# Pairwise interaction tower on one core: products stored so that both halves of the embedding share partitions, an accumulating DMA per group of products, and one column sum in TensorE instead of two

## The chip, the cores and the metric

The kernel runs on 1 core of one Trainium2 chip. The metric is device time in microseconds, the median of several runs. TensorE (PE) multiplies matrices, VectorE (DVE) does the elementwise products, ScalarE (ACT) copies out of PSUM, GpSimd (POOL) and SyncE (SP) issue DMAs, which 16 DMA engines carry out.

## The reference, cut to what matters

```python
e = jnp.stack([tbl_0[ids[:, 0]], ..., tbl_39[ids[:, 39]]], axis=1)   # 512 x 40 x 64
vi, vj = e[:, i_idx, :], e[:, j_idx, :]                              # all 780 pairs i < j
viW = jnp.einsum('bpd,pde->bpe', vi, W)                              # W: 780 x 64 x 64
z = jnp.einsum('bpe,bpe->bp', viW, vj)                               # 512 x 780
h = jnp.concatenate([z, dense_ctx], axis=1)                          # + 16
h = jnp.maximum(h @ W_top1 + b_top1, 0.0)                            # 796 -> 512
h = jnp.maximum(h @ W_top2 + b_top2, 0.0)                            # 512 -> 256
y = h @ W_top3                                                       # 256 -> 1
```

All is float32. For each pair of fields the kernel forms W'e_i, multiplies it elementwise by e_j and sums over the 64 dimensions of the embedding.

## The kernel before, in words

The batch of 512 lies along the free axis everywhere. The 40 fields are taken as 20 pairs of fields. The pair of fields 2k and 2k+1 is called k, and u = 19 - k is the order in which they arrive. `E[:, k, :]` holds both, transposed: one field on partitions 0 to 63 and the other on 64 to 127.

The first two arrivals are looked up on TensorE with one-hot codes (small tables). The other 18 are fetched by POOL, with eight indirect DMAs each (2 fields x 4 slices of the batch), into a ring of four buffers `rows`. TensorE transposes them into `ps_e` (L388), and ACT copies `ps_e` to `E` (L288).

The 780 pairs are packed into 100 groups of 8 pairs (a few with gaps). A group has two steps. A step is two matmuls (L408, `products`) from 64 partitions of `w_sb` and `E` into two banks of `ps_t`. The two run side by side, on the upper and the lower half of the array. Each gives 128 rows: two pairs of fields with 64 dimensions each. `ps_t` has room for STEPS = 3 steps. DVE multiplies each step by `E` into `prod` (L355, `multiply`), one instruction of 128 x 1024.

The sum over the embedding is then a matmul with a matrix of ones and zeros (L420, `reduce`): four matmuls of 128 rows and 32 columns per group, one for each 512 columns of `prod`, which go side by side to the four quarters of the partitions of `ps_z`. Sixteen groups fill a chunk of `ps_z`, which ACT copies to `z`. There are 7 chunks, the last of 4 groups.

The order of the work on TensorE is a list written by `order()`: after the products of every odd group n, `reduce(n-3)` and `reduce(n-2)` follow, and the transposes of an arrival stand one group ahead of the first group that needs it. SP loads weights (`w_sb`, 256 KB for two groups, ring of 12) and the parameters of the top layers. POOL does nothing but the gathers. After the last group the top layers run on TensorE (L446, L464, L470), with the last two reductions among the matmuls of L446.

Of the kernel before, what the change touches and what calls it, by code (L numbers as in the profile page):

```python
# [16 lines left out]
DIM = 64  # L34
DENSE = 16
PAIRS = FIELDS * (FIELDS - 1) // 2
KP = FIELDS // 2
SP_ = KP // 2
# [7 lines left out]
G_RING = 4  # L46
W_RING = 12
P_RING = 4
STEPS = 3


def pair(i, j):

    return i * FIELDS - i * (i + 1) // 2 + j - i - 1


def plan_groups():


    groups = []  # L60
    for k in reversed(range(KP)):
        for M in range(k // 2 + 1, SP_):
            groups.append((k, [(i, (pair(i, 2 * m), pair(i, 2 * m + 1)), m)
                               for m in (2 * M, 2 * M + 1) for i in (2 * k, 2 * k + 1)]))
        if k % 2 == 0:

            own = [(2 * k, (None, pair(2 * k, 2 * k + 1)), k),
                   (2 * k + 3, (pair(2 * k + 2, 2 * k + 3), None), k + 1)]
            cross = [(i, (pair(i, 2 * k + 2), pair(i, 2 * k + 3)), k + 1) for i in (2 * k, 2 * k + 1)]
            groups.append((k, own + cross))  # L70

    groups.insert(3, groups.pop(0))
    return groups
# [10 lines left out]
AHEAD = 1  # L84
PARAMS_AT = 12


def arrival(k):

    return KP - 1 - k  # L90


def first_group(u):

    return next((n for n, (k, _) in enumerate(GROUPS) if arrival(k) >= u), NG)
# [6 lines left out]
def place(u):  # L102

    return SPLIT_FIRST.index(u) if u < FIRST else u


def order():

    u = 0
    for n in range(NG):  # L110
        while u < KP and first_group(u) - AHEAD <= n:
            yield "fields", u
            u += 1
        yield "group", n


def table_split(rows):

    used = max(d for d in range(1, P + 1) if rows % d == 0)
    return used, rows // used  # L120


def tower_kernel(nc, w_units, ids, ids_by_field, tables, dense, w1, b1, w2, b2, w3, out):
    with ExitStack() as ctx:
# [15 lines left out]
        halves = sb("halves", [P, 2 * (2 * PER_CHUNK - 1)])  # L140
# [3 lines left out]
        prod = sb("prod", [P, P_RING, BLOCKS, BATCH])  # L144

        scratch = prod[:].rearrange("p a b n -> p (a b n)")
# [41 lines left out]
        halves_zeroed = sem("halves_zeroed")  # L188
        halves_ready = sem("halves_ready")
        rows_loaded = [sem(f"rows_loaded{i}") for i in range(G_RING)]  # L190
        transposed = sem("transposed")
        e_copied = sem("e_copied")
        w_loaded = [sem(f"w_loaded{i}") for i in range(W_RING)]
        step_done = sem("step_done")
        product_ready = sem("product_ready")
        group_reduced = sem("group_reduced")
# [10 lines left out]

# [46 lines left out]
        @block.gpsimd  # L254
        def _(pool):
            pool.memset(ident[:], 0.0).then_inc(ident_zeroed, 1)
            pool.wait_ge(ident_zeroed, 1)
            pool.affine_select(out=ident[:], in_=ident[:], compare_op=ALU.not_equal, fill=1.0, base=0,
                               pattern=[[-1, P]], channel_multiplier=1).then_inc(ident_ready, 1)
            for i, f in enumerate(looked_up):  # L260
                pool.iota(first_row[:, i:i + 1], pattern=[[0, 1]], base=0,
                          channel_multiplier=splits[f][1]).then_inc(first_row_ready, 1)
            pool.wait_ge(ids_loaded, 16)

            def gather(u):
# [12 lines left out]
            for u in range(LOOKED_UP, KP):  # L278
                gather(u)

        @block.scalar
        def _(act):
            def copy_fields(u):
                if u < LOOKED_UP:
# [3 lines left out]
                act.activation(E[:, KP - 1 - u, :], e_bank[u], ACT.Copy).then_inc(e_copied, 1)  # L288

            def copy_z(c):  # L290
                if c < CHUNKS - 1:
                    act.wait_ge(group_reduced, PER_CHUNK * (c + 1))
                    act.activation(z[:, c, :], ps_z[:], ACT.Copy).then_inc(z_copied, 1)  # L293
                else:
                    act.wait_ge(group_reduced, NG)
                    top = 32 * (BLOCKS - 1)
                    act.activation(z[0:top, c, :], ps_z[0:top, :], ACT.Copy).then_inc(z_copied, 1)
# [3 lines left out]
            for kind, at in order():  # L301
                if kind == "fields":
                    if at >= FIRST:
                        copy_fields(at)
                elif at % 2 == 1 and (at - 1) % PER_CHUNK == 0 and at > 1:
                    copy_z(at // PER_CHUNK - 1)
            copy_z(CHUNKS - 1)
# [11 lines left out]
        def _(dve):  # L319
            dve.memset(halves[:], 0.0).then_inc(halves_zeroed, 1)  # L320
            mid = 2 * (PER_CHUNK - 1)
            dve.wait_ge(halves_zeroed, 1)
            dve.memset(halves[0:DIM, mid:mid + 1], 1.0).then_inc(halves_ready, 1)
            dve.memset(halves[DIM:P, mid + 1:mid + 2], 1.0).then_inc(halves_ready, 1)

# [5 lines left out]

# [10 lines left out]
            def multiply(n):  # L342
                slot = n % P_RING
                if n >= P_RING:
                    dve.wait_ge(group_reduced, n - P_RING + 1)
                blocks = GROUPS[n][1]
                for s in range(2):
                    m0, m1 = blocks[2 * s][2], blocks[2 * s + 1][2]
                    dve.wait_ge(e_copied, max(place(arrival(m)) for m in (m0, m1)) + 1)
                    dve.wait_ge(step_done, 2 * n + s + 1)  # L350
                    if m0 == m1:
                        multiplier = E[:, m0, None, :].to_broadcast([P, 2, BATCH])
                    else:
                        multiplier = E[:, m0:m0 + 2, :]
                    dve.tensor_tensor(prod[:, slot, 2 * s:2 * s + 2, :], ps_t[:, (2 * n + s) % STEPS, :, :], multiplier,  # L355
# [6 lines left out]
            dve.wait_ge(group_reduced, NG)  # L362
# [5 lines left out]
        def _(pe):  # L368
            def look_up_fields(u):

                before = sum(len(codes_of) for codes_of in code_list[:u])
                for j, (f, c) in enumerate(code_list[u], start=before):
                    if u == 1 and j - before in FETCHED_AT:
                        transpose_fields(LOOKED_UP + FETCHED_AT.index(j - before))
                    if c == 0:
# [3 lines left out]
                    last = pe.matmul(e_bank[u][half:half + DIM, :], small[f][:, c, :],  # L379
                                     codes[0:splits[f][0], j % CODE_RING, :],  # L380
                                     start=(c == 0), stop=(c == splits[f][1] - 1)).then_inc(code_used, 1)
# [10 lines left out]
            def products(n):  # L392
# [3 lines left out]
                k, blocks = GROUPS[n]  # L396
                pe.wait_ge(e_copied, max(place(arrival(i // 2)) for i, _, _ in blocks) + 1)
                for s in range(2):
                    step = 2 * n + s

# [4 lines left out]
                    for j in range(2):  # L405
                        i = blocks[2 * s + j][0]
                        at, col = i % 2 * DIM, (n % 2 * 2 + s) * P
                        last = pe.matmul(ps_t[:, step % STEPS, j, :], w_sb[at:at + DIM, m % W_RING, col:col + P],  # L408
                                         E[at:at + DIM, i // 2, :], start=True, stop=True)
                    last.then_inc(step_done, 1)  # L410

            def reduce(n):

                pe.wait_ge(product_ready, 2 * n + 2)
                c, q = divmod(n, PER_CHUNK)
                if c >= 1 and q == 0:
                    pe.wait_ge(z_copied, c)
                at = 2 * (PER_CHUNK - 1 - q)
                for b in range(BLOCKS):
                    last = pe.matmul(ps_z[32 * b:32 * b + 32, :], halves[:, at:at + 32],  # L420
                                     prod[:, n % P_RING, b, :], start=(q == 0),
                                     stop=(q == PER_CHUNK - 1 or n == NG - 1))
                last.then_inc(group_reduced, 1)

            pe.wait_ge(ident_ready, 1)
            pe.wait_ge(halves_ready, 2)
            for u in range(LOOKED_UP):
                look_up_fields(u)
            for kind, at in order():
# [9 lines left out]
            pe.wait_ge(params_loaded, 16 * (CHUNKS + 5))  # L439
            pe.wait_ge(z_copied, CHUNKS - 1)  # L440
            pe.wait_ge(e_copied, KP)
# [33 lines left out]
def z_rows():  # L475

    at = np.full((CHUNKS, P), -1)
    for n, (_, blocks) in enumerate(GROUPS):
        for b, (_, halves, _) in enumerate(blocks):
            for h, p in enumerate(halves):  # L480
                if p is not None:
                    at[n // PER_CHUNK, 32 * b + 2 * (n % PER_CHUNK) + h] = p
    at[CHUNKS - 1, DENSE_AT:DENSE_AT + DENSE] = PAIRS + np.arange(DENSE)
    return at
# [42 lines left out]
```

## Time and profile before

| | |
|---|---|
| median of 3 runs | 361.19 us (360.8 to 361.52) |
| the profiled execution, its own time | 361.39 us |
| its span, first to last instruction | 359.4 us |
| granted clock of TensorE | 1.000 |
| PE busy | 343.5 us (96%) |
| DVE busy | 249.4 us (69%) |
| POOL busy | 139.4 us (39%) |
| ACT busy | 22.1 us (6%) |

Busy time is the time in which at least one instruction of the engine ran; one matmul of float32 stands as two records. The span is some 2 us shorter than the time that is measured. Windows and timelines count from the first instruction.

### The profile page before, as it was taken

To read this page: it belongs to the slowest core of one execution; us is meant where nothing else is said; L and a number is where in the kernel's file an instruction comes from. 1 tells how busy PE (TensorE), PEld (TensorE's weight loads), DVE (VectorE), ACT (ScalarE), POOL (GpSimd) and SP (SyncE) were. 2 spreads that over 40 slices of the span, in tenths; PEclk is the share of its full clock that TensorE was granted. 3 is DMA by queue.
4 is the path that set the end of the run, shared out by engine and by line. 5 is a ranking of instruction groups with operands and counts; after the bars stand their busy time and mean duration, and the time that the engine had idled before them with its cause. 6 is when DMAs were issued, how large, how long until landed. Compare 5 with 4: busy or idle time off the path is not lost.

```text
span 359.4 us, 4510 instructions
## 1 busy us (share of the span) xinstructions
PE 343.5 (96%) x1824; PEld 117.6 (33%) x1824; DVE 249.4 (69%) x243; ACT 22.1 (6%) x35; POOL 139.4 (39%) x154
## 2 busy tenths in 40 slices
PE   0799998999999999999999999999999999999997
PEld 0233332333332333333333333333333332333342
DVE  2384977687879787878888788787878979870000
ACT  1011000000000000000000000000000000000032
POOL 6777777777777777772343500000000000000000
DMA  6972222222233239322131220212000000000000
GB/s 167 256 215 63 83 57 58 83 60 84 55 86 63 80 96 308 88 55 75 40 78 45 71 60 29 60 30 60 29 0 2 0 2 0 0 3 0 0 2 0
DMA packets 14399, 22.87 MB, mean 64 GB/s; under 512 B 3750, under 2 KB 3878, under 8 KB 14379
## 3 DMA queue, kind: packets, MB, share of 16 engines
q1 hardware_dynamic: 9770, 17.86, 16.5%
q0 software_dynamic: 4608, 4.73, 6.2%
q8 instruction: 15, 0.25, 0.3%
q14 instruction: 6, 0.04, 0.0%
HBM read 22.57 MB, written 0.00 MB: 63 GB/s over the span
## 4 chain that ended last, share of the span: by engine, by line
PE 80%; POOL 13%; issue 4%; DMA 1%; DVE 1%; ACT 0%; DVEq 0%
PE ps_t L408 45%; PE ps_z L420 24%; POOL rows L273 13%; PE ps_t L446 5%; PE ps_e L388 2%; PE ps_t L464 2%; PE ps_e L446 2%; DVE prod L355 1%; DMA rows<-in_tbl,ids_sb 1%; DMA ids_sb<-in_ids_t 1%; PE ps_t L470 1%; ACT y_sb L316 0%; DVEq L350 0%
## 5 line engine op out<-in xcount | busy, mean ns | idle before, releaser
L355 DVE TENSOR_TENSOR prod<-ps_t,E 128x1024 f32<-128x1024 f32 x200 | 231.7, 1216 | 60.1 <-PE ps_t L408 58.9
L408 PE MATMUL ps_t<-E,w_sb 64*128 64x512 f32 x800 | 189.2, 606 | 0.2
L273 POOL DMA_INDIRECT rows<-in_tbl,ids_sb x144 | 138.4, 961 | 63.9 <-issue 43.0
L408 PEld LDWEIGHTS ps_t<-E,w_sb 64*128 64x128 f32 x800 | 69.5, 186 | 109.7 <-issue 80.0
L420 PE MATMUL ps_z<-prod,halves 128*32 128x512 f32 x800 | 96.4, 598 | 0.0
L420 PEld LDWEIGHTS ps_z<-prod,halves 128*32 128x32 f32 x800 | 20.8, 109 | 68.0 <-DVE prod L355 34.9
L288 ACT ACTIVATE E<-ps_e 128x512 f32<-128x512 f32 x18 | 10.8, 598 | 231.7 <-PE ps_e L388 209.7
L338 DVE TENSOR_SCALAR prod<-prod,first_row_f 125x512 f32<-125x512 int32 x38 | 16.5, 495 | 11.8 <-PE ps_e L379 5.8
L379 PE MATMUL ps_e<-prod 125*64 125x512 f32 x40 | 12.8, 728 | 11.2 <-DMA prod<-in_tbl 11.2
L446 PE MATMUL ps_t<-z,w_sb 128*128 128x512 f32 (+1 forms) x42 | 18.7, 597 | 0.0
L388 PE MATMUL ps_e<-ident,rows 128*128 128x128 f32 x68 | 11.1, 286 | 2.3 <-DMA rows<-in_tbl,ids_sb 2.3
L364 DVE COPY z<-ps_z 8x512 f32<-8x512 f32 x1 | 0.7, 697 | 17.6 <-PE ps_z L420 17.6
L388 PEld LDWEIGHTS ps_e<-ident,rows 128*128 128x128 f32 x68 | 7.1, 141 | 15.8 <-issue 10.9
L446 PEld LDWEIGHTS ps_t<-z,w_sb 128*128 128x128 f32 (+1 forms) x42 | 7.8, 190 | 10.8 <-issue 10.8
L379 PEld LDWEIGHTS ps_e<-prod 125*64 125x64 f32 x40 | 3.5, 166 | 19.6 <-issue 14.3
L379 PE MATMUL ps_t<-prod 125*64 125x512 f32 x36 | 9.0, 596 | 0.0
L293 ACT ACTIVATE z<-ps_z 128x512 f32<-128x512 f32 x6 | 3.6, 597 | 66.6 <-PE ps_z L420 66.6
L464 PE MATMUL ps_t<-E,w_sb 128*128 128x512 f32 x16 | 7.0, 592 | 0.0
L446 PE MATMUL ps_e<-z,w_sb 128*128 128x512 f32 (+1 forms) x14 | 6.4, 600 | 0.0
L464 PEld LDWEIGHTS ps_t<-E,w_sb 128*128 128x128 f32 x16 | 3.0, 190 | 3.8 <-issue 3.8
L379 PEld LDWEIGHTS ps_t<-prod 125*64 125x64 f32 x36 | 2.7, 137 | 4.9 <-issue 3.5
L446 PEld LDWEIGHTS ps_e<-z,w_sb 128*128 128x128 f32 (+1 forms) x14 | 2.6, 190 | 3.7 <-issue 3.7
(22 smaller groups left out, 12.6 us busy)
## 6 DMA issues: line engine op xcount, KB each, us to landing
w_sb<-in_w_units SPq DMA_DIRECT2D x50, 256.0 KB, 2.6
rows<-in_tbl,ids_sb POOLq DMA_INDIRECT x144, 2.5
w_sb<-in_w SPq DMA_DIRECT2D x7, 256.0 KB
prod<-in_ids_by_field SPq DMA_DIRECT2D x2, 512.0 KB, 9.0
prod<-in_tbl SPq DMA_DIRECT2D x3, 312.5 KB
w_sb<-in_w SPq DMA_DIRECT2D x1, 512.0 KB
prod<-in_tbl SPq DMA_DIRECT2D x1, 250.0 KB
ids_sb<-in_ids_t SPq DMA_DIRECT2D x1, 80.0 KB, 1.8
```

What stands on the lines that cost most here:

```text
L273: pool.indirect_dma_start(rows[:, g % G_RING, b, f * DIM:(f + 1) * DIM], None, tables[2 * k + f], bass.IndirectOffsetOnAxis(ap=ids_sb[:, c ...
L288: act.activation(E[:, KP - 1 - u, :], e_bank[u], ACT.Copy).then_inc(e_copied, 1)
L293: act.activation(z[:, c, :], ps_z[:], ACT.Copy).then_inc(z_copied, 1)
L338: dve.tensor_scalar(codes[0:used, j % CODE_RING, :], ids_wide[0:used, i, :], float(c), first_row_f[0:used, i:i + 1], ALU.subtract, ALU.is_ ...
L355: dve.tensor_tensor(prod[:, slot, 2 * s:2 * s + 2, :], ps_t[:, (2 * n + s) % STEPS, :, :], multiplier, ALU.mult).then_inc(product_ready, 1)
L379: last = pe.matmul(e_bank[u][half:half + DIM, :], small[f][:, c, :], codes[0:splits[f][0], j % CODE_RING, :], start=(c == 0), stop=(c == s ...
L388: last = pe.transpose(e_bank[u][:, b * P:(b + 1) * P], rows[:, (u - LOOKED_UP) % G_RING, b, :], ident[:])
L408: last = pe.matmul(ps_t[:, step % STEPS, j, :], w_sb[at:at + DIM, m % W_RING, col:col + P], E[at:at + DIM, i // 2, :], start=True, stop=True)
L420: last = pe.matmul(ps_z[32 * b:32 * b + 32, :], halves[:, at:at + 32], prod[:, n % P_RING, b, :], start=(q == 0), stop=(q == PER_CHUNK - 1 ...
L446: last = pe.matmul(h1_bank[m], w1_sb[0:used, c, m * P:(m + 1) * P], z[0:used, c, :], start=(c == 0), stop=(c == CHUNKS - 1))
L464: last = pe.matmul(h2_bank[m], w2_sb[:, c, m * P:(m + 1) * P], h1[:, c, :], start=(c == 0), stop=(c == H1 // P - 1))
L470: last = pe.matmul(y_bank[0:1, :], w3_sb[:, c:c + 1], h2[:, c, :], start=(c == 0), stop=(c == H2 // P - 1))
```

## The change

The products are laid out anew. For an ordinary group (k, M), which pairs the fields 2k and 2k+1 with the four fields 4M to 4M+3, step 0 now makes dimensions 0 to 31 of all four products, and step 1 dimensions 32 to 63, on the same 128 partitions. So the two halves of a product stand at the same partitions of `prod[:, slot, 0]` and `prod[:, slot, 1]`. The multiplier must have the same layout, so a new tensor `E4` is filled from `E` by four small DMAs (32 partitions x 2 KB) per arrival, issued by ACT behind its copy. `E` itself becomes a ring of 6.

For 76 of the 100 groups (`ADDED`: ordinary ones from 10 to 91), POOL issues an accumulating DMA that adds half 1 to half 0 in `prod`, 512 KB read and added to 512 KB. TensorE then sums only `prod[:, slot, 0]`: two matmuls for the group and not four. The groups (k, None), which hold the pairs within a block of four fields, keep the old layout and sums, as does TensorE for the groups outside `ADDED` (two sums each).

Reductions are now taken by two groups at a time (`reduce_two`), so that the matmuls of two groups stand side by side in the four quarters of `ps_z`. Both being in `ADDED` (35 of the 50 twos), four matmuls do; else (6 twos with one in it, 9 with none) a second round for half 1 follows. `reduce_two(n-7)` follows the products of odd n (before: n-3 and n-2), and `prod` has 8 slots for 4. POOL's gathers are issued between the adds, twelve groups ahead.

```diff
-P_RING = 4
+P_RING = 8
+LAG = 7
+GATHER_LEAD = 12
+ADDED = [n for n, (_, M) in enumerate(GROUPS) if M is not None and 10 <= n < 92]
...
-        E = sb("E", [P, KP, BATCH])
+        E = sb("E", [P, E_RING, BATCH])
+        E4 = sb("E4", [P, QUADS, 2, BATCH])
...
-            for u in range(LOOKED_UP, KP):
-                gather(u)
+            def add_halves(n):
+                pool.wait_ge(product_ready, 2 * n + 2)
+                pool.dma_start(prod[:, n % P_RING, 0, :, :], prod[:, n % P_RING, 1, :, :],
+                               accum_op=ALU.add).then_inc(halves_added[n % P_RING], 16)
+
+            u = LOOKED_UP
+            for n in range(NG):
+                while u < KP and first_group(u) <= n + GATHER_LEAD:
+                    gather(u)
+                    u += 1
+                if n in ADDED:
+                    add_halves(n)
...
-                act.activation(E[:, KP - 1 - u, :], e_bank[u], ACT.Copy).then_inc(e_copied, 1)
+                if u >= E_RING:
+                    act.wait_ge(product_ready, 2 * last_group(u - E_RING) + 2)
+                    act.wait_ge(e4_placed[u - E_RING], 64)
+                act.activation(E[:, slot_of(k), :], e_bank[u], ACT.Copy).then_inc(e_copied, 1)
+                if k < 2:
+                    return
+                act.wait_ge(e_copied, place(u) + 1)
+                for f in range(2):
+                    for h in range(2):
+                        to, of = (2 * (k % 2) + f) * HALF, f * DIM + h * HALF
+                        act.dma_start(E4[to:to + HALF, k // 2, h, :], E[of:of + HALF, slot_of(k), :]).then_inc(
+                            e4_placed[u], 16)
...
-                    if at > 1 and at % 2 == 1:
-                        reduce(at - 3)
-                        reduce(at - 2)
+                    if at >= LAG and at % 2 == 1:
+                        reduce_two(at - LAG)
...
+            def reduce_two(n):
+                c, q = divmod(n // 2, PER_CHUNK // 2)
+                if c >= 1 and q == 0:
+                    pe.wait_ge(z_copied, c)
+                for g in (n, n + 1):
+                    pe.wait_ge(product_ready, 2 * g + 2)
+                    if g in ADDED:
+                        pe.wait_ge(halves_added[g % P_RING], 16 * sum(a % P_RING == g % P_RING for a in ADDED if a <= g))
+                for s in range(2):
+                    for g in (n, n + 1):
+                        if s == 1 and g in ADDED:
+                            continue
+                        if GROUPS[g][1] is None:
+                            ones = halves[:, 30 - 4 * q - 2 * s:62 - 4 * q - 2 * s]
+                        else:
+                            ones = quads[:, 28 - 4 * q:60 - 4 * q]
+                        for j in range(2):
+                            to = 32 * (2 * (g % 2) + j)
+                            last = pe.matmul(ps_z[to:to + 32, :], ones, prod[:, g % P_RING, s, j, :],
+                                             start=(q == 0 and s == 0),
+                                             stop=((q == PER_CHUNK // 2 - 1 or n == NG - 2)
+                                                   and (s == 1 or g in ADDED)))
+                last.then_inc(two_reduced, 1)
...
-            sum_h1(0, 0, CHUNKS - 1)
-            reduce(NG - 2)
-            for m in range(1, 3):
-                sum_h1(m, 0, CHUNKS - 1)
-            reduce(NG - 1)
-            for m in range(3, H1 // P):
+            reduce_two(NG - 6)
+            pe.wait_ge(params_loaded, 16 * (CHUNKS + 5))
+            pe.wait_ge(z_copied, CHUNKS - 2)
+            pe.wait_ge(e_copied, KP)
+            sum_h1(0, 0, CHUNKS - 2)
+            reduce_two(NG - 4)
+            sum_h1(0, CHUNKS - 2, CHUNKS - 1)
+            pe.wait_ge(product_ready, 2 * NG - 2)
+            sum_h1(1, 0, CHUNKS - 1)
+            reduce_two(NG - 2)
+            for m in range(2, H1 // P):
                 sum_h1(m, 0, CHUNKS - 1)
```

The first groups are reordered, too: (16, None) and (18, None) now stand first; they don't read `E4`. An arrival u is first needed by group 16 (u = 8), 20 (u = 9), 25 (u = 10), and so on to 90 (u = 19), as before.

## Rows read from the trace of the kernel before

**Rows 1.** The page: busy time, share of the span and instructions of each engine.

```profile
PE 343.5 (96%) x1824; PEld 117.6 (33%) x1824; DVE 249.4 (69%) x243; ACT 22.1 (6%) x35; POOL 139.4 (39%) x154
```

**Rows 2.** The chain that ended last, in order of time: start us, us, what.

```profile
64.03 2.34 DMA rows<-in_tbl,ids_sb
...
68.99 1.85 PE ps_z L420 x16
70.84 3.63 PE ps_t L408 x16
...
321.85 5.35 PE ps_e L446 x12
```

**Rows 3.** Groups of instructions by line: out<-in, shapes, count | busy us, mean ns | idle before.

```profile
L355 DVE TENSOR_TENSOR prod<-ps_t,E 128x1024 f32<-128x1024 f32 x200 | 231.7, 1216 | 60.1 <-PE ps_t L408 58.9
L408 PE MATMUL ps_t<-E,w_sb 64*128 64x512 f32 x800 | 189.2, 606 | 0.2
...
L420 PE MATMUL ps_z<-prod,halves 128*32 128x512 f32 x800 | 96.4, 598 | 0.0
```

**Rows 4.** Stretches: length, PE, PEld, DVE, ACT and POOL busy, clock, DMA share, GB/s.

```profile
67.00:100.00 33.00, 33.00 (x195) 11.19 (x196) 25.64 (x23) 2.39 (x4) 25.00 (x27) 1.00 0.27 73
100.00:200.00 100.00, 99.93 (x578) 34.12 (x578) 80.02 (x70) 4.78 (x8) 61.07 (x65) 1.00 0.33 91
200.00:321.80 121.80, 121.74 (x713) 40.46 (x709) 100.47 (x88) 4.19 (x7) 3.09 (x4) 1.00 0.08 24
321.80:359.40 37.60, 35.35 (x96) 13.90 (x92) 1.08 (x2) 5.30 (x8) 0.00 (x0) 1.00 0.00 0
```

**Rows 5.** Timeline around 200 us: start us, us, engine, line, operation, count, idle before.

```profile
204.51 4.62 DVE L355 TENSOR_TENSOR prod<-ps_t,E 128x1024 f32<-128x1024 f32 x4 [0.87 <-PE ps_t L408]
```

**Rows 6.** Timeline of POOL: last gather of u = 7, first of 8, first and last of 9.

```profile
64.03 0.94 POOL L273 DMA_INDIRECT rows<-in_tbl,ids_sb  x1 [0.30 <-issue]
65.27 0.95 POOL L273 DMA_INDIRECT rows<-in_tbl,ids_sb  x1 [0.30 <-issue]
...
75.26 0.94 POOL L273 DMA_INDIRECT rows<-in_tbl,ids_sb  x1 [0.30 <-issue]
...
83.99 0.94 POOL L273 DMA_INDIRECT rows<-in_tbl,ids_sb  x1 [0.30 <-issue]
```

**Rows 7.** Timeline of PE and ACT: products of groups 16 and 17, then a reduction.

```profile
66.41 0.66 PE L388 MATMUL ps_e<-ident,rows 128*128 128x128 f32 x4 [0.85 <-DMA rows<-in_tbl,ids_sb]
...
82.53 3.70 PE L408 MATMUL ps_t<-E,w_sb 64*128 64x512 f32 x16
...
86.17 1.92 PE L420 MATMUL ps_z<-prod,halves 128*32 128x512 f32 x16
```

**Rows 8.** The gathers (min/median/max ns, first to last start) and their landing.

```profile
L273 POOL DMA_INDIRECT rows<-in_tbl,ids_sb x144: 938/944/1305, 2.9 to 203.1; - x144
...
DMA to landing us min/median/max: 2.3/2.5/6.7
```

**Rows 9.** The page: DMA queues, and DMA issues with KB each and us to landing.

```profile
q1 hardware_dynamic: 9770, 17.86, 16.5%
q0 software_dynamic: 4608, 4.73, 6.2%
...
w_sb<-in_w_units SPq DMA_DIRECT2D x50, 256.0 KB, 2.6
```

**Rows 10.** SP's issues of the weights (min/median/max ns).

```profile
L240 SPq DMA_DIRECT2D w_sb<-in_w_units x50: 327/328/3710, 4.2 to 252.8; - x50
```

**Rows 11.** Timeline of the first products: ACT's copy of the last of four arrivals, and DVE.

```profile
34.05 0.60 ACT L288 ACTIVATE E<-ps_t 128x512 f32<-128x512 f32 x1 [1.26 <-PE ps_t L379]
...
35.19 9.14 DVE L355 TENSOR_TENSOR prod<-ps_t,E 128x1024 f32<-128x1024 f32 x8 [4.82 <-PE ps_t L408]
```

More of the change, by code:

```diff
@@ L34 @@
 DIM = 64
+HALF = DIM // 2
 DENSE = 16
@@ L61, in plan_groups @@
     for k in reversed(range(KP)):
-        for M in range(k // 2 + 1, SP_):
-            groups.append((k, [(i, (pair(i, 2 * m), pair(i, 2 * m + 1)), m)
-                               for m in (2 * M, 2 * M + 1) for i in (2 * k, 2 * k + 1)]))
+        groups += [(k, M) for M in range(k // 2 + 1, QUADS)]
         if k % 2 == 0:
[L67 to L73, printed above, removed]
+            groups.append((k, None))
+    first = [(KP - 4, None), (KP - 2, None)]
+    return first + [g for g in groups if g not in first]
 GROUPS = plan_groups()
@@ L81, with pairs_of, last_group @@
 DENSE_AT = 32 * (BLOCKS - 1) + LAST_ROWS
-AHEAD = 1
-PARAMS_AT = 12
+ADDED = [n for n, (_, M) in enumerate(GROUPS) if M is not None and 10 <= n < 92]
 def arrival(k):
     return KP - 1 - k
+def pairs_of(n):
+    k, M = GROUPS[n]
+    return [[k, k], [k, k]] if M is not None else [[k + 1, k], [k, k]]
 def first_group(u):
     return next((n for n, (k, _) in enumerate(GROUPS) if arrival(k) >= u), NG)
+def last_group(u):
+    return max(n for n in range(NG) for ks in pairs_of(n) for k in ks if arrival(k) == u)
 SPLIT_FIRST = (0, 2, 3, 1)
@@ L104, in place, with slot_of @@
     return SPLIT_FIRST.index(u) if u < FIRST else u
+def slot_of(k):
+    return arrival(k) % E_RING
 def order():
@@ L192, in tower_kernel @@
         e_copied = sem("e_copied")
+        e4_placed = [sem(f"e4_placed{u}") for u in range(KP)]
         w_loaded = [sem(f"w_loaded{i}") for i in range(W_RING)]
@@ L195, in tower_kernel @@
         product_ready = sem("product_ready")
-        group_reduced = sem("group_reduced")
+        halves_added = [sem(f"halves_added{i}") for i in range(P_RING)]
+        two_reduced = sem("two_reduced")
         z_copied = sem("z_copied")
@@ L304, in _ @@
                         copy_fields(at)
-                elif at % 2 == 1 and (at - 1) % PER_CHUNK == 0 and at > 1:
-                    copy_z(at // PER_CHUNK - 1)
-            copy_z(CHUNKS - 1)
+                elif at % 2 == 1 and at > LAG and (at - LAG + 2) % PER_CHUNK == 0:
+                    copy_z((at - LAG) // PER_CHUNK)
+            copy_z(CHUNKS - 2)
+            act.wait_ge(two_reduced, NU)
+            top = 32 * (BLOCKS - 1)
+            act.activation(z[0:top, CHUNKS - 1, :], ps_z[0:top, :], ACT.Copy).then_inc(z_copied, 1)
             act.wait_ge(params_loaded, 16 * (CHUNKS + 5))
@@ L342, in multiply @@
             def multiply(n):
-                slot = n % P_RING
+                k, M = GROUPS[n]
                 if n >= P_RING:
-                    dve.wait_ge(group_reduced, n - P_RING + 1)
-                blocks = GROUPS[n][1]
-                for s in range(2):
-                    m0, m1 = blocks[2 * s][2], blocks[2 * s + 1][2]
-                    dve.wait_ge(e_copied, max(place(arrival(m)) for m in (m0, m1)) + 1)
-                    dve.wait_ge(step_done, 2 * n + s + 1)
[L351 to L355, printed above, removed]
+                    dve.wait_ge(two_reduced, (n - P_RING) // 2 + 1)
+                if M is None:
+                    dve.wait_ge(e_copied, max(place(arrival(k)), place(arrival(k + 1))) + 1)
+                elif k == 2 * M - 1:
+                    for m in (2 * M, 2 * M + 1):
+                        dve.wait_ge(e4_placed[arrival(m)], 64)
+                for s in range(2):
+                    if M is not None:
+                        multiplier = E4[:, M, s, None, :].to_broadcast([P, 2, BATCH])
+                    elif s == 0:
+                        multiplier = E[:, slot_of(k + 1):slot_of(k + 1) + 2, :]
+                    else:
+                        multiplier = E[:, slot_of(k + 1), None, :].to_broadcast([P, 2, BATCH])
+                    dve.wait_ge(step_done, 2 * n + s + 1)
+                    dve.tensor_tensor(prod[:, n % P_RING, s, :, :], ps_t[:, (2 * n + s) % STEPS, :, :], multiplier,
                                       ALU.mult).then_inc(product_ready, 1)
@@ L378, in look_up_fields @@
                     half = f % 2 * DIM
[L379 to L381 removed]
+                    pe.matmul(e_bank[u][half:half + DIM, :], small[f][:, c, :],
+                              codes[0:splits[f][0], j % CODE_RING, :],
+                              start=(c == 0), stop=(c == splits[f][1] - 1)).then_inc(code_used, 1)
             def transpose_fields(u):
@@ L395, in products @@
                     pe.wait_ge(w_loaded[m % W_RING], 16 * (m // W_RING + 1))
-                k, blocks = GROUPS[n]
-                pe.wait_ge(e_copied, max(place(arrival(i // 2)) for i, _, _ in blocks) + 1)
+                pe.wait_ge(e_copied, max(place(arrival(k)) for ks in pairs_of(n) for k in ks) + 1)
                 for s in range(2):
@@ L410, in products @@
                     last.then_inc(step_done, 1)
-            def reduce(n):
-                pe.wait_ge(product_ready, 2 * n + 2)
-                c, q = divmod(n, PER_CHUNK)
+            def reduce_two(n):
+                c, q = divmod(n // 2, PER_CHUNK // 2)
                 if c >= 1 and q == 0:
                     pe.wait_ge(z_copied, c)
[L418 to L423, printed above, removed]
+                for g in (n, n + 1):
[8 more added lines that the diff above has]
+                            ones = halves[:, 30 - 4 * q - 2 * s:62 - 4 * q - 2 * s]
+                        else:
+                            ones = quads[:, 28 - 4 * q:60 - 4 * q]
[6 more added lines that the diff above has]
+                last.then_inc(two_reduced, 1)
@@ L477, in z_rows, with weight_index @@
     at = np.full((CHUNKS, P), -1)
[L478 to L482, printed above, removed]
-    at[CHUNKS - 1, DENSE_AT:DENSE_AT + DENSE] = PAIRS + np.arange(DENSE)
+    for n, (k, M) in enumerate(GROUPS):
+        for j in range(2):
+            row = at[n // PER_CHUNK, 32 * (2 * (n % 2) + j) + 4 * (n // 2 % (PER_CHUNK // 2)):][:4]
+            if M is not None:
+                row[:] = [pair(2 * k + j, 4 * M + t) for t in range(4)]
+            else:
+                row[1 - j] = pair(2 * k + 2, 2 * k + 3) if j == 0 else pair(2 * k, 2 * k + 1)
+                row[2:] = [pair(2 * k + j, 2 * k + 2), pair(2 * k + j, 2 * k + 3)]
+    at[CHUNKS - 1, DENSE_AT:DENSE_AT + DENSE] = PAIRS + np.arange(DENSE)
+    return at
+def weight_index():
+    d, e = np.arange(DIM)[:, None], np.arange(DIM)[None, :]
+    at = np.full((NG, 2, 2, DIM, P), PAIRS * DIM * DIM)
+    for n, (k, M) in enumerate(GROUPS):
+        for j in range(2):
+            if M is not None:
+                for s in range(2):
+                    for t in range(4):
+                        at[n, s, j, :, t * HALF:(t + 1) * HALF] = (
+                            pair(2 * k + j, 4 * M + t) * DIM * DIM + d * DIM + (e + s * HALF))[:, :HALF]
+            else:
+                for t in range(2):
+                    at[n, 1, j, :, t * DIM:(t + 1) * DIM] = pair(2 * k + j, 2 * k + 2 + t) * DIM * DIM + d * DIM + e
+        if M is None:
+            at[n, 0, 0, :, DIM:] = pair(2 * k + 2, 2 * k + 3) * DIM * DIM + d * DIM + e
+            at[n, 0, 1, :, :DIM] = pair(2 * k, 2 * k + 1) * DIM * DIM + e * DIM + d
     return at
```

59 lines of the change are left out of this document (26 added, 33 removed).

## The prediction, on record before the result was known

> **What bounds the kernel now.** I read the page first: TensorE is busy for 343.5 of 359.4 us, DVE for 249.4, POOL for 139.4 [rows 1]. The stretches say where that holds: from 67 us to the end of the groups at 321.8 us TensorE never rests, DVE is busy for about 80% of it, and POOL is in use only up to 203 us [rows 4, 8]. By line, products and reductions take 189.2 and 96.4 us of TensorE's time [rows 3]; the change thins the second. The chain shows the rhythm: 3.63 us for the products of two groups, 1.85 us for their two reductions, so 5.48 us for two groups [rows 2]. Ahead of 67 us the last thing waited for is a gather (2.34 us from issue to landing, until 66.4) [rows 2, 7]. DVE needs 4.62 us for the four multiplications of two groups, 1.155 us each, and then idles 0.87 us until TensorE has made more [rows 5]. So TensorE is the bound by 0.86 us in every two groups, and DVE stands right behind it. That 0.86 us, not the time of the matmuls taken out, is what a lighter TensorE can give.
>
> **The change part by part.** *The reductions.* Two groups now take 8 matmuls in 1.85 us, which run four abreast: 0.925 us a round. Where both are added (35 twos of 50) one round goes: TensorE needs 3.63 + 0.925 = 4.56 us. DVE needs 4.62, and sets the pace. The twos with one added group or none (15) keep both rounds and 5.48 us. Gain: 35 x (5.48 - 4.62) = 30.1 us. Had TensorE alone set it, 32.4. The three banks of ps_t let DVE run on meanwhile: of 3 x 1.155 = 3.47 us per turn of a bank, DVE's 1.155 and TensorE's 0.91 leave 1.4 us, more than the 0.925 of a round, so I take no bubble.
>
> *The adds on POOL.* A DMA issued by POOL is in the trace only as a gather: 0.94 us and 0.30 us to the next, 1.25 us each [rows 6, 8]. An add also has 128 rows, so I take 1.25 us. Bounds: 0.33 us, what SP spends on a plain issue [rows 10], and 2.5 us, twice a gather, if source and target are each described in two pieces. In all, POOL gets 76 x 1.25 = 95 us on top of its 80 gathers from u = 10 on (100 us).
>
> *Landing.* A 256 KB load lands 2.6 us after issue [rows 9]. On q1 a megabyte takes 0.165 x 16 x 359.4 / 17.86 = 53 us of one engine [rows 9], so a further 256 KB on 16 engines is 0.87 us: an add lands 3.4 to 3.5 us after its issue begins, if it costs as a plain copy.
>
> *First wait.* POOL takes its work in order, and the gathers of u = 8 and 9 stand ahead of the add of group 10. They end at 84.9 us [rows 6]. Nothing on TensorE has changed till then, so it comes to the reduction of 10 and 11 at 86.2 us [rows 7]. Their adds start at 85.2 and 86.5 and the second lands at 89.9: 3.7 us are lost. TensorE reduces (to 90.8), makes the products of 18 and 19 with four transposes between (3.63 + 0.66, to 95.1) and wants 12 and 13. The add of 12 starts at 87.7, but ahead of that of 13 stands the gather of u = 10, eight issues or 10.0 us: it starts at 99.0 and lands at 102.4. 7.3 us are lost, together 11.0. With half the landing time it would be some 2 us less.
>
> *Later waits.* Nine more gathers (u = 11 to 19) stand ahead of adds. Reductions lag seven groups: from the end of a product to its reduction TensorE does three twos, 13.9 us, of which DVE's own lag of some 1.6 us must go: 12.3 us. An add that becomes ready as a gather of 10.0 us begins waits for that, for the add of its partner (1.25) and for its landing (3.4): 14.7 us, 2.4 us late. If it becomes ready later in the gather it is in time. POOL's backlog from the start makes it worse for some, and a stall moves TensorE back and makes the next one less likely. I take 1 us each, 9 us, between 0 and 22 (nine times 2.4).
>
> *Check by POOL alone.* From 85 us: 100 + 95 us ends at 280; landing, and what follows the reduction of 90 and 91 (0.9; products of 98 and 99, 3.6; reductions from 92 to 95, 3.7; the 37.6 us after the last group [rows 4]) gives 280 + 3.4 + 45.8 = 329 us of span. TensorE without waits: 359.4 - 30.1 = 329.3. Two equally long chains that wait for each other end later than either; that is why the waits cost.
>
> *The DMA engines.* This is the dispute. An add writes 0.524 MB; as a plain copy it takes 53 x 0.524 / 16 = 1.74 us of all 16 engines. If the read of its target counts like another copy it is 3.5 us. What else they have from 85 us on is 47 us (shares of [rows 4] times their stretches, less 0.27 of the 18 us before 85) and some 9 us for E4 (40 DMAs of 64 KB). So the engines are done at 85 + 56 + 76 d, and the span is 187 + 76 d. At d = 1.74 it is 319: hidden. It reaches today's 359.4 at d = 2.27. I take 1.74, the row of the nearest thing that is seen; 3.5 stays as a rival.
>
> A rule of the Trainium skill speaks against this. Its page *Collectives: The Full Stack*, section "The bandwidth ceiling", says that a reduce in the DMA engines runs at about half the rate of a copy, for its two source reads pass through one ring. No row here shows it. By that rule d is 3.5 us at the trace's rate and, as an estimate with the 435 GB/s that the Trainium skill's *SBUF — State Buffer* gives (section "Door 1"), 2.4 us: spans of 453 and 370 us.
>
> *What costs nothing.* ACT's four issues per arrival, at SP's 0.33 us [rows 10], are 1.3 us behind a copy of 0.60 [rows 11]; ACT is busy 6% and a copy of z comes 3.6 us before TensorE needs its room. Uncovered, 18 times 1.3 would be 23 us. The first wait for E4: ACT's copy ends at 34.65, the last of four issues lands by about 38.3; groups 0 and 1 keep DVE from 35.2 to 39.8 [rows 11], so it is covered by 1.5 us. Gathers behind adds: asked twelve groups ahead (28 us), they need 12.3. The ring of six E buffers waits for products at least six groups old. The tail has the same matmuls in another order: 0. Memsets at the start: a few tenths beside the loads.
>
> *Sum.* 361.2 - 30.1 + 11.0 + 9 = 351.1 us. I made the terms against the profiled execution (361.4, span 359.4), which lies 0.2 us above the median; 351 is the forecast, and its own range is 338 to 360.
>
> **The rivals.** *The DMA engines become the bound (slower).* The place is every reduction of added groups from about group 16 on, each waiting for halves_added; the price is d, and it decides from 2.27 us. For it: an add has two inputs, and half of the copy rate is nothing odd. Against it: the engines stand at 8 to 33% [rows 4], and 4 KB per row may do better than the 1.83 KB mean packet of the row. At d = 2.8, between 2.3 and 3.5, the span is 400 and the time 402; at 3.5 it is 455.
>
> *POOL's issue is dearer (slower).* With p per add POOL alone gives 85 + 100 + 76 p + 49.2, or 234 + 76 p: 359.4 at p = 1.65. At 2 us it is 386, time 388. Against it: gathers with as many rows and an index list on top take 0.94 [rows 8].
>
> *The waits are absorbed (faster still).* If an issue costs 0.33 to 1.0 us, POOL is free between gathers; the later waits vanish and the first shrink to some 8: 361.2 - 30.1 + 0 to 8 = 331 to 338.
>
> *It does nothing.* DVE stands 0.86 us per two groups behind; waits of 30 us in all, or d of 2.3, would eat exactly the gain: 361.
>
> **How the numbers follow.** Forecast (338 to 360) 0.40; absorbed (331 to 338) 0.13; DMA engines 0.31, spread from 362 to 455; POOL's issue 0.11, from 362 to 395; nothing 0.05. Faster by over 0.2% (about what a measurement of this kernel can tell from no change): 0.53; within: 0.05; slower: 0.42. The range runs from 332 to 412: below it 0.06, above it that part of the DMA rival that has d over 2.9, 0.13.
>
> **What would show it.** TensorE's x8 rounds of L420's successor at 0.93 us, and DVE busy for over 90% between 110 and 300 us, confirm the gain. The waits of TensorE or its weight loads for "DMA prod" price the rest: 11 us between 86 and 104 us and about 1 us per gather if I am right; more than 1 us at nearly every reduction if the DMA engines bind, with their share of the time above 0.9. The add's own row on POOL gives p, and its time to landing gives 3.4 us or more. I am wrong if p is over 1.5 or the landing over 6 us in the middle of the span: each microsecond of landing beyond the 12.3 us of slack is paid in full at every gather.

## The result, and the profile after

The change makes the kernel slower: 385.71 us against 361.36 us, a ratio of 1.067 (95% interval 1.061 to 1.073). The forecast was 351. What came is the rival with the DMA engines as the bound, whose own figure was 402 in a spread from 362 to 455. The profiled execution is the fastest of four (383.83 to 387.27 us); its span is 382.0 us.

From the page of the changed kernel: busy times; then TensorE's granted clock, DMA share and GB/s in 40 slices; the queues (packets, MB, share of 16 engines); the chain by line; the DMA issues with the time to landing.

```profile
PE 322.1 (84%) x1520; PEld 112.6 (29%) x1520; DVE 250.3 (66%) x248; ACT 22.2 (6%) x35; POOL 208.6 (55%) x230
...
PEclk9999989996899999989999999999989999999999
DMA  6864543439799999999999999999999999900000
GB/s 176 251 213 114 130 110 79 108 86 196 137 228 219 230 228 243 255 253 264 242 256 241 223 227 232 235 231 226 234 220 203 188 196 202 177 2 0 0 0 0
...
q0 software_dynamic: 15552, 44.58, 59.4%
q1 hardware_dynamic: 9770, 17.86, 15.2%
...
POOL rows L265 31%; DMA prod<-prod 21%; PE ps_t L421 11%; PE ps_z L443 7%; DVE prod L372 5%; PE ps_t L465 5%; POOL prod L272 5%; PE ps_t L488 2%; PE ps_e L465 2%; PE ps_e L404 1%; DMA ids_sb<-in_ids_t 0%; PE ps_t L494 0%; ACT y_sb L328 0%; 
...
prod<-prod POOLq DMA_DIRECT2D x76, 512.0 KB, 13.5
w_sb<-in_w_units SPq DMA_DIRECT2D x50, 256.0 KB, 8.4
```

TensorE lost work, 343.5 to 322.1 us [rows 1], but it now idles. The row to read is that of the DMA share: from the twelfth slice to the 35th it stands at 9. The add that was to land in 3.4 us lands in 13.5, and the weights' load went from 2.6 [rows 9] to 8.4. The packets of q0 took 0.594 x 16 engines x 382.0 us. Divided by 16 that is 226.9 us; the gathers' share before was 0.062 x 359.4 = 22.3 us [rows 9]. What is left for 76 adds is 204.6 us, or **2.69 us of all 16 engines for each**, where the sum had 1.74. (In the runs without adds below the gathers take 22.4 to 23.7 us, so this step is good to about 0.02 us.)

The stretches (length, then busy time of PE, PEld, DVE, ACT and POOL, clock, DMA share, GB/s) and the waits (total us, times, longest) show what that does:

```profile
100.00:150.00 50.00, 42.59 (x212) 14.92 (x212) 36.79 (x33) 2.39 (x4) 37.62 (x41) 0.97 1.06 222
150.00:200.00 50.00, 37.49 (x188) 12.78 (x188) 34.05 (x30) 1.80 (x3) 27.68 (x30) 0.97 1.07 256
200.00:250.00 50.00, 42.64 (x222) 14.85 (x216) 38.60 (x34) 1.80 (x3) 29.52 (x32) 1.00 1.05 231
250.00:300.00 50.00, 44.26 (x224) 15.07 (x222) 40.48 (x36) 1.80 (x3) 28.73 (x32) 0.97 1.04 219
...
PE ps_z L443 <- DMA prod<-prod: 42.3, 21, 7.4
```

Before, TensorE was busy for 99.93 of the 100 us from 100 on [rows 4]; now it is for 80. Nearly all of its idle time ahead of the sums, 42.3 of 42.5 us, ends with an add that lands. A DMA share above 1, as in these stretches, can only come from packets whose times overlap. So the 2.69 us are packet time, and the engines got through a little more than that suggests. The chain shows something else besides: the adds go out in bunches, five together after eight gathers.

```profile
142.34 0.95 POOL rows L265
...
147.04 1.71 POOL prod L272 x2
148.75 19.09 DMA prod<-prod
```

The second of these adds lands 19.09 us after the end of its issue. The first wait stands on the timeline (start, length, engine, line, count, idle before and its releaser):

```profile
84.86 2.80 POOL L272 DMA_DIRECT2D prod<-prod  x3
87.96 1.08 POOL L265 DMA_INDIRECT rows<-in_tbl,ids_sb  x1 [0.30 <-issue]
93.50 1.94 PE L443 MATMUL ps_z<-prod,quads 128*32 128x512 f32 x8 [7.38 <-DMA prod<-prod]
97.85 3.68 POOL L272 DMA_DIRECT2D prod<-prod  x4
```

Place and order are as forecast (wait for 10 and 11, then a gather ahead of 13), but the first wait is 7.4 and not 3.7 us, with three adds of 2.7 us under way at once. With plain copies in their place (below) the same wait is 4.3 us. After the idle time TensorE's clock has dropped: the same round of four matmuls (x8) takes 1.94 us here and 1.06 elsewhere, close to the ratio of its two levels (1.2 and 2.4 GHz), and the granted clock is 0.90 from 67 to 100 us. It was 1.00 throughout before [rows 4].

### The profile page after: what moved, and what is told of

The parts are those of the page before. It is cut to its first block, busy times and chain, and to the rows that moved or that the text cites. A ratio compares the mean times of both kernels' runs of the same rounds, so it can differ in the third digit from the quotient of the medians.

```text
span 382.0 us, 4053 instructions
## 1 busy us (share of the span) xinstructions
PE 322.1 (84%) x1520; PEld 112.6 (29%) x1520; DVE 250.3 (66%) x248; ACT 22.2 (6%) x35; POOL 208.6 (55%) x230
## 3 DMA queue, kind: packets, MB, share of 16 engines
q0 software_dynamic: 15552, 44.58, 59.4%
## 4 chain that ended last, share of the span: by engine, by line
POOL 35%; PE 27%; DMA 21%; issue 11%; DVE 5%; ACT 0%; DVEq 0%
POOL rows L265 31%; DMA prod<-prod 21%; PE ps_t L421 11%; PE ps_z L443 7%; DVE prod L372 5%; PE ps_t L465 5%; POOL prod L272 5%; PE ps_t L488 2%; PE ps_e L465 2%; PE ps_e L404 1%; DMA ids_sb<-in_ids_t 0%; PE ps_t L494 0%; ACT y_sb L328 0%; DVEq L371 0%
## 5 line engine op out<-in xcount | busy, mean ns | idle before, releaser
L421 PE MATMUL ps_t<-E,w_sb 64*128 64x512 f32 x800 | 193.0, 618 | 0.6 <-ACT E L294 0.5
L265 POOL DMA_INDIRECT rows<-in_tbl,ids_sb x144 | 140.2, 974 | 44.6 <-issue 43.5
L421 PEld LDWEIGHTS ps_t<-E,w_sb 64*128 64x128 f32 x800 | 72.7, 191 | 113.8 <-issue 90.2
L272 POOL DMA_DIRECT2D prod<-prod x76 | 67.4, 1171 | 70.0 <-DVE prod L372 70.0
L443 PE MATMUL ps_z<-prod,quads 128*32 128x512 f32 x416 | 61.9, 632 | 42.5 <-DMA prod<-prod 42.3
L443 PEld LDWEIGHTS ps_z<-prod,quads 128*32 128x32 f32 x416 | 10.5, 110 | 81.5 <-DVE prod L372 51.9
L443 PE MATMUL ps_z<-prod,halves 128*32 128x512 f32 x80 | 17.2, 598 | 0.0
L404 PEld LDWEIGHTS ps_e<-ident,rows 128*128 128x128 f32 x68 | 7.1, 140 | 16.9 <-issue 10.9
L465 PEld LDWEIGHTS ps_t<-z,w_sb 128*128 128x128 f32 (+1 forms) x42 | 7.9, 190 | 10.4 <-issue 10.4
L443 PEld LDWEIGHTS ps_z<-prod,halves 128*32 128x32 f32 x80 | 3.4, 109 | 8.7 <-issue 6.4
## 6 DMA issues: line engine op xcount, KB each, us to landing
prod<-prod POOLq DMA_DIRECT2D x76, 512.0 KB, 13.5
```

Of the source, the lines that this page charges most:

```text
L265: pool.indirect_dma_start(rows[:, g % G_RING, b, f * DIM:(f + 1) * DIM], None, tables[2 * k + f], bass.IndirectOffsetOnAxis(ap=ids_sb[:, c ...
L272: pool.dma_start(prod[:, n % P_RING, 0, :, :], prod[:, n % P_RING, 1, :, :], accum_op=ALU.add).then_inc(halves_added[n % P_RING], 16)
L404: last = pe.transpose(e_bank[u][:, b * P:(b + 1) * P], rows[:, (u - LOOKED_UP) % G_RING, b, :], ident[:])
L443: last = pe.matmul(ps_z[to:to + 32, :], ones, prod[:, g % P_RING, s, j, :], start=(q == 0 and s == 0), stop=((q == PER_CHUNK // 2 - 1 or n ...
L465: last = pe.matmul(h1_bank[m], w1_sb[0:used, c, m * P:(m + 1) * P], z[0:used, c, :], start=(c == 0), stop=(c == CHUNKS - 1))
```

## The experiments

Two theories went in. D: the adds fill the DMA engines. P: the order on POOL (eight gathers in a row ahead of adds) costs the time. Times are medians, ratios against the kernel before in the same runs.

**No adds.** `ADDED` is empty, nothing is left out of the sums.

```diff
-ADDED = [n for n, (_, M) in enumerate(GROUPS) if M is not None and 10 <= n < 92]
+ADDED = []
```

> The changed kernel with no accumulating DMA: TensorE sums both halves of every group, all else of the change (layout, E4 and its DMAs, ring of six for E, reductions by twos, lag of seven) stays. Theory D (the adds fill the DMA engines: about 2.7 us of all 16 for each) and theory P (POOL's order puts gathers ahead of adds) both expect TensorE's pace of before, 5.48 us for two groups: 360 to 363 us, DMA share as before plus a few hundredths for E4. A theory L (the new layout, E4's DMAs or the rings cost something by themselves) expects over 365 us.

364.21 us, 1.0078 (1.0061 to 1.0094). Neither theory's figure: 2.9 us over before. The new layout with all its small DMAs nearly comes free; the 2.9 us are taken up again below (reductions after three groups).

**A plain copy in place of the add.**

```diff
-                pool.dma_start(prod[:, n % P_RING, 0, :, :], prod[:, n % P_RING, 1, :, :],
-                               accum_op=ALU.add).then_inc(halves_added[n % P_RING], 16)
+                pool.dma_start(prod[:, n % P_RING, 0, :, :], prod[:, n % P_RING, 1, :, :]).then_inc(halves_added[n % P_RING], 16)
```

> The 76 DMAs on POOL copy half 1 over half 0 and don't add (the output is without one half of those products): same issues, same bytes written, same waits, one read fewer. Theory D: about 1.5 to 1.75 us of all 16 engines for each, which is less than TensorE and DVE need for a group (2.31), so 345 to 358 us and landings of 4 to 6 us in the middle. Theory P expects what the changed kernel measures, 380 to 390 us, for the order on POOL is the same.

350.97 us, 0.971 (0.965 to 0.976). From its page, the queue and the issues:

```profile
q0 software_dynamic: 15552, 44.58, 36.2%
...
prod<-prod POOLq DMA_DIRECT2D x76, 512.0 KB, 5.5
```

Same packets, same megabytes, same order on POOL, and 35 us less. (0.362 x 348.8 - 22.3) / 76 = 1.37 us for a copy; the add takes 1.96 times that. Theory P, which had both the same, is out as the main cause.

**A small add.** 128 of 1024 elements of each row are added; the rest of half 1 is lost.

```diff
-                pool.dma_start(prod[:, n % P_RING, 0, :, :], prod[:, n % P_RING, 1, :, :],
+                pool.dma_start(prod[:, n % P_RING, 0, 0, 0:128], prod[:, n % P_RING, 1, 0, 0:128],
```

> The 76 adds take only 128 of the 1024 elements of a row, 64 KB each (the rest of half 1 is left out of the sums): POOL issues as much and in the same order, the DMA engines get an eighth of the bytes. Theory D: 340 to 352 us, what the forecast's sum without the DMA engines gave (351) or less, with landings of 2.5 to 3.5 us. Theory P: above 375 us.

349.35 us, 0.968 (0.966 to 0.970), q0 at 18.9%: 0.57 us of the engines for 64 KB. An add of few bytes is cheap, so it is not the accumulating DMA as such that costs. POOL's longer issue of an add (0.9 us against 0.55 for a copy) is no main cause either: this run has it.

**Half 1 left out, no adds.**

```diff
-                if n in ADDED:
-                    add_halves(n)
...
-                    if g in ADDED:
-                        pe.wait_ge(halves_added[g % P_RING], 16 * sum(a % P_RING == g % P_RING for a in ADDED if a <= g))
```

> No adds, no waits for them, and TensorE leaves half 1 of the 76 groups out of the sums all the same: the gain of the change without its price. If DVE's 4.62 us for two groups sets the pace where a round is gone, 361.4 - 30.1 = 331 us (327 to 335) with DVE over 90% busy from 110 to 290 us. If the rings or E4 bind instead, it stays above 340 us.

333.85 us, 0.925 (0.923 to 0.927). Its stretch of 180 us in the middle:

```profile
110.00:290.00 180.00, 180.00 (x936) 62.19 (x936) 169.15 (x147) 7.78 (x13) 56.55 (x60) 1.00 0.26 72
```

DVE is busy for 94%, so it does set the pace where a round is gone. Its busy times, which the account at the end needs:

```profile
PE 313.1 (94%) x1520; PEld 109.5 (33%) x1520; DVE 249.8 (75%) x248; ACT 22.1 (7%) x35; POOL 139.1 (42%) x154
```

Against e1, 364.21 - 333.85 = 30.4 us: the gain term of the sum was 30.1.

**Half of the bytes.** The add takes 512 of 1024 elements; the other 512 of half 1 are lost.

```diff
-                pool.dma_start(prod[:, n % P_RING, 0, :, :], prod[:, n % P_RING, 1, :, :],
+                pool.dma_start(prod[:, n % P_RING, 0, 0, :], prod[:, n % P_RING, 1, 0, :],
```

> The 76 adds take 512 of the 1024 elements of a row, 256 KB each (the other 512 of half 1 are left out). Issues and order on POOL as in the changed kernel. If the price is bytes on the DMA engines with two reads, an add takes half of the 2.7 us of the changed kernel, 1.3 to 1.4 us, as the plain copy of 512 KB did (1.37), and the time is that of the plain copy, 347 to 354 us. If an accumulating packet cost by itself and not by its bytes, it stays over 370 us.

355.77 us, 0.984 (0.980 to 0.989), q0 at 40.1%: 1.56 us for 256 KB. With 0.57 for 64 KB and 2.8 for 512 KB (below) the price is about 0.25 us and 0.5 us for each 100 KB. It is somewhat over the 1.3 to 1.4 expected. The time is at the upper end of the expected 347 to 354 or above it: the four runs are 354.04, 354.15, 357.39 and 360.13 us, a wider spread than elsewhere.

**Fewer adds.** Adds for two of every three twos, nothing left out (e6, 53 adds, 25 twos with one round); and the same without those ahead of group 20 (e7, 45 adds, 21 such twos).

```diff
+ADDED = [n for n in ADDED if n // 2 % 3 != 1]
```

For e7:

```diff
-ADDED = [n for n, (_, M) in enumerate(GROUPS) if M is not None and 10 <= n < 92]
+ADDED = [n for n, (_, M) in enumerate(GROUPS) if M is not None and 20 <= n < 92]
+ADDED = [n for n in ADDED if n // 2 % 3 != 1]
```

> Adds only for the twos of groups with n // 2 % 3 != 1: 53 adds, 25 twos with one round, nothing left out. Theory D: 53 x 2.7 = 143 us of the engines no longer bind; the gain is 25 x 0.86 = 21.5 us less the wait at the start (8 to 12 us, POOL's order), less 3 us of the later reductions and some waits: 350 to 358 us. If the engines are still in the way it stays over 362.

> As e6, but no add before group 20: 45 adds, 21 twos with one round. It takes away the adds that stand behind the gathers of u = 9 and 10. If that wait costs the 8 to 11 us at 86 to 104 us, this is faster than e6 by 8 less the four twos given up (3.4 us): 345 to 352 us. If it costs nothing, it is slower than e6 by 3 us.

367.48 us, 1.016 (1.014 to 1.018), and 357.04 us, 0.990 (0.987 to 0.992). Both missed their ranges, e6 by 9 us and e7 by 5, and e6's engines are not even full: shares of 0.79 to 0.97 from 110 to 260 us. I put it down to bunching, which e11 below tests: behind the first gathers three adds go out at once, and at 2.8 us each the last one lands over 8 us later. At e6's first two waits:

```profile
85.15 2.81 POOL L273 DMA_DIRECT2D prod<-prod  x3
93.70 1.94 PE L444 MATMUL ps_z<-prod,quads 128*32 128x512 f32 x8 [7.16 <-DMA prod<-prod]
103.40 1.76 PE L444 MATMUL ps_z<-prod,quads 128*32 128x512 f32 x8 [2.75 <-DMA prod<-prod]
```

9.9 us in two waits. e7, which has no adds there, is 10.4 us faster though it gives up four one-round twos (3.4 us). It still has 7.5 us of waits for adds (two, the longer 5.8).

**Reductions after three groups.** As e1, with `LAG = 3`. The tail's calls of `reduce_two(NG - 6)` and `reduce_two(NG - 4)` and ACT's last `copy_z` behind the loop are taken out, since the loops reach them.

```diff
-LAG = 7
+LAG = 3
...
-ADDED = [n for n, (_, M) in enumerate(GROUPS) if M is not None and 10 <= n < 92]
+ADDED = []
...
-            copy_z(CHUNKS - 2)
...
-            reduce_two(NG - 6)
...
-            reduce_two(NG - 4)
```

> As e1 (no adds, nothing left out), with the reductions three groups behind the products as before, and not seven. e1 was 2.9 us slower than the kernel before. If that is because four groups more are reduced after the last product, and not while TensorE waits for gathers ahead of 67 us (four groups are 3.7 us), this gives 361 to 362 us, as before. If E4 or the other layout costs it, it stays at 364.

360.43 us, 0.9971 (0.9960 to 0.9982): the 2.9 us are gone, and 1.2 more (the kernel before took 361.60 in these runs), a little under the 361 to 362 expected. Ahead of 66 us, e1's timeline has two reductions and e8's has four, as before:

```profile
54.99 1.93 PE L443 MATMUL ps_z<-prod,halves 128*32 128x512 f32 x16
61.07 1.92 PE L443 MATMUL ps_z<-prod,quads 128*32 128x512 f32 x16
```

```profile
42.40 1.92 PE L442 MATMUL ps_z<-prod,halves 128*32 128x512 f32 x16
49.74 1.92 PE L442 MATMUL ps_z<-prod,quads 128*32 128x512 f32 x16
55.23 1.92 PE L442 MATMUL ps_z<-prod,quads 128*32 128x512 f32 x16
61.84 1.92 PE L442 MATMUL ps_z<-prod,quads 128*32 128x512 f32 x16
```

In that stage TensorE waits for gathers, and a reduction there costs nothing. A lag of seven moves two of them behind the last product, where each microsecond counts.

**Gathers one by one.** `singles` lists, for each arrival u from 10 on, its eight DMAs, number i at n = first_group(u) - GATHER_LEAD - 1 + i; those of u = 2 to 9 go out ahead of the loop. `gather(u, [i])` issues DMA number i alone. e9 has all adds, e10 plain copies, e11 the adds of e7, and e12 those of every other two from group 20 on (33 adds, 15 twos with one round).

```diff
-            u = LOOKED_UP
+            singles = [(max(first_group(u) - GATHER_LEAD - 1 + i, 0), u, i) for u in range(10, KP) for i in range(8)]
+            for u in range(LOOKED_UP, 10):
+                gather(u)
             for n in range(NG):
-                while u < KP and first_group(u) <= n + GATHER_LEAD:
-                    gather(u)
-                    u += 1
+                for at, u, i in singles:
+                    if at == n:
+                        gather(u, [i])
                 if n in ADDED:
                     add_halves(n)
```

> The changed kernel with POOL's gathers from u = 10 on issued one by one, one after each group, and not eight in a row; all 76 adds stay, nothing is left out. Theory D (adds of 2.7 us each fill the engines): order doesn't help where the engines are full, 374 to 386 us. Theory P (order and bunching cost the time): 350 us or less, as with the plain copy or better.

> The same spreading with plain copies for adds (half 0 of those products is lost). With engines free, what is left over the 334 us of e4 in the plain copy's 351 us should be POOL's order: this gives 334 to 342 us. If it stays at 348 or more, the waits of e2 and e3 come from something else than the eight gathers in a row.

> e7 (45 adds, from group 20 on, two twos of three) with the gathers spread. Three twos take TensorE and DVE 14.7 us, and 4 adds of 2.8 us with the loads of three twos some 14 us of the engines: nearly full. Sum 361.3 + 2.9 - 21 x 0.86 = 346; with some waits left, 347 to 354 us, and faster than e7 (357) by 3 to 9.

> 33 adds, from group 20 on, every other two (15 twos with one round), gathers spread. The engines have 5.6 us of adds and 2 to 3 us of loads in each 10.1 us, so no wait should be left: 361.3 + 2.9 - 15 x 0.86 = 351 us (350 to 353). If two of three (e11) is at its sum of 346, that is the better; if its engines are full, this is.

| | us | ratio (95%) | without the spreading |
|---|---|---|---|
| e9, 76 adds | 385.03 | 1.066 (1.064 to 1.068) | 385.71 |
| e10, 76 plain copies | 341.09 | 0.945 (0.943 to 0.946) | 350.97 |
| e11, 45 adds | 346.35 | 0.960 (0.956 to 0.963) | 357.04 |
| e12, 33 adds | 351.70 | 0.974 (0.972 to 0.975) | |

This separates the two. Where the engines are full (e9) the order on POOL changes nothing; where they are not, it is worth 10 us: the plain copies stand 17.1 us above e4 without the spreading and 7.2 with it. The stretch from 110 to 290 us of e9, with two of its waits, and then that of e11:

```profile
110.00:290.00 180.00, 151.44 (x732) 52.55 (x728) 133.19 (x115) 6.57 (x11) 116.93 (x119) 0.94 1.06 236
PE ps_z L447 <- DMA prod<-prod: 22.5, 12, 6.5
...
PE ps_e L408 <- DMA rows<-in_tbl,ids_sb: 19.5, 9, 3.6
```

```profile
110.00:290.00 180.00, 180.00 (x984) 62.07 (x984) 159.86 (x139) 7.79 (x13) 105.08 (x107) 1.00 0.93 202
```

In e9 the waits moved and did not go. TensorE waits for adds for 22.5 us and no longer 42.3. It now waits for 19.5 us for gathers, which was 3.5 in the changed kernel. With the engines full, what is issued one by one lands late as well: a gather lands 8.3 us after its issue (median), against 5.5 in the changed kernel and 2.5 before [rows 8].

e11 is the version to keep: right in all sums, 4.0% faster than before. Its TensorE never idles in the middle, at a DMA share of 0.93, and its time is its sum: 361.3 + 2.9 - 21 x 0.86 = 346.1, 0.7 us better than the range given for it. Against e7, whose adds it has, TensorE's idle time falls from 28.3 to 17.3 us and its busy time hardly moves (326.6 and 327.3). Its queue row gives (0.431 x 344.6 - 22.3) / 45 = 2.80 us for an add, that of e12 (33.1% of 349.6 us, 33 adds) 2.83. It keeps the lag of seven; whether the 2.9 us can be had back with adds wasn't tried.

## Why the prediction was wrong

**The step that failed** is the one called the dispute: "I take 1.74, the row of the nearest thing that is seen". An add took 2.69 us of all engines here, 2.8 where they had slack. A copy took 1.37. So 1.74 was too dear for what it described and too cheap for what it was used for. The nearest row was that of a plain load, and an add costs about twice a copy of the same bytes. That took it past the break-even, worked out there as d = 2.27, and the sign turned. The rival's line, 187 + 76 d, gives 391 us of span at 2.69, and 382.0 was measured, 9 us less. The line takes a share of 1 as full; the packets of 100 to 300 us add up to shares of 1.04 to 1.07, which is 11 us more than the 200 us themselves. That is the size of the difference.

**The rule's factor came out.** The Trainium skill (*Collectives: The Full Stack*, "The bandwidth ceiling") has a reduce at half the rate of a copy, for its two reads. Measured here, inside one core's SBUF: 2.69 to 2.83 against 1.37 us, a factor of 1.96 to 2.07. The factor is shown (e2) and so is that the price grows with the bytes (e3, e5). That it is the second read, and not the adding itself, no run here separates: the queue's row has the same 44.58 MB for adds and copies. If both reads count, 2 x 0.524 MB in 2.80 us are an estimated 374 GB/s, some 14% under the 435 GB/s of the Trainium skill's *SBUF — State Buffer* (section "Door 1").

**Right:** the bound and the gain (30.1 us forecast, 30.4 between e1 and e4); DVE's 4.62 us as the pace; that a layout with E4 hides (e1 and e8). ACT's issues cost more than SP's row said, 0.61 (median) and not 0.33 us each, and were still hidden. The place of the first wait and the gather ahead of group 13 were right, too.

**Right in sum by luck, off in parts:** with d out of the way, the forecast of 351 is what the plain copy measures, 350.97. That they agree to 0.1 us is luck, since errors both ways cancel. By parts: the lag's 2.9 us were missing ("The tail has the same matmuls in another order: 0" looked at the tail alone, and not at where its two reductions had been hidden); the waits were 20 us, and 350.97 - (361.3 + 2.9 - 30.1) leaves 16.9. Of these only 11.0 are idle time (TensorE idles for 29.9 us in e2 and 18.9 in e4); the other 5.8 are the same matmuls taking longer (318.9 against 313.1 us busy), for which the sum had no term. The issue on POOL was 1.25 us and is 0.93 for an add (2.80 for three; 67.4 us for all 76) and 0.55 for a copy: the rival "POOL's issue is dearer" is out. The rival "absorbed" ends by its own sum at 339 and not 338.

**The account of the changed kernel.** e4 has the same matmuls and no adds, so its profile is the measure: 332.0 us of span against 382.0. TensorE idles for 18.9 us there and 59.9 here. That is 41.0 us more, about the 42.3 us of waits for adds. It is busy for 313.1 us there and 322.1 here, 9.0 us more for the same 1520 records. The two make up the 50.0 us. The 9.0 us fit TensorE's granted clock, 0.973 over the span against 1.000 in e4, and matmuls after each longer wait at up to nearly twice their time. That is read from rows; no run keeps the waits and holds the clock.

**Chances.** Slower had 0.42 against 0.53. What spoke against the rival, "4 KB per row may do better than the 1.83 KB mean packet", was true of copies (0.524 MB in 1.37 us is 383 GB/s, where 1.74 us would be 301) and could not make up for a factor of two.

## What to carry to other kernels

Price a DMA by the bytes that it reads and writes together with its op: an accumulating one cost the engines twice a copy here. Add up the engines' time for the busiest stretch and compare it with the stretch itself: here 76 adds of 2.7 us alone, 205 us, filled the 82 groups of 2.3 to 2.7 us in which they stood, before any load was counted. Where a shared resource is nearly full, use it for part of the work (two of three here) and space out what goes into it: eight short DMAs issued in a row turned the long ones behind them into a bunch, and the last of a bunch set the wait. And when work is put off to give something time, look at which idle time it had been filling.

## What the runs showed of the hardware

- An accumulating DMA of float32 from SBUF to SBUF, 128 rows of 4 KB each: 2.7 to 2.8 us of the 16 engines, a plain one 1.37 (383 GB/s). Of 2 KB each 1.56, of 512 bytes 0.57.
- POOL spends some 0.9 us to issue such an add and 0.55 us for the plain copy; an indirect gather takes 0.94 and 0.30 to the next. ACT spends 0.61 us on each small plain DMA (median of 72 in e1; four in 2.44 us) where SP's issues take 0.33 [rows 10].
- After a wait of 7.4 us TensorE's matmuls ran at about half speed for a few microseconds (1.94 us for a round that takes 1.06; the granted clock of the stretch from 67 to 100 us is 0.90), though the engine had been busy without a break for some 19 us before it (67 to 86 us).
- With the engines' share above 1 everything that used them landed later: an add after 13.5 us, a 256 KB load after 8.4 (2.6 before [rows 9]), and in e9 a gather after 8.3 (2.5 before [rows 8]).
